# New places for the small pieces of work in a software-pipelined attention block, and value products spread over three rounds

## The chip, the cores and the metric

The kernel runs on one core of a Trainium2 chip. The metric is the device time of one execution in microseconds (us). The kernel before was timed three times: 1149.63, 1153.11 and 1153.94 us, so the median is 1153.11 us.

## The reference, cut to what matters

The input is 16 sequences of 512 tokens with 128 features. A block of attention is followed by a block of experts:

```python
x = x + layernorm(attention(layernorm(x)))        # 16 heads of 8 features, causal
x = x + layernorm(experts(layernorm(x)))          # 1 shared unit of 256, 8 routed experts of 128, top 2

# attention, for each of the 16 heads
scores = (einsum('bhqd,bhkd->bhqk', Q, K) + einsum('bhqd,qkd->bhqk', Q, rel_k[idx])) / sqrt(8)
attn = softmax(where(causal, scores, -1e9))
out = einsum('bhqk,bhkd->bhqd', attn, V) + einsum('bhqk,qkd->bhqd', attn, rel_v[idx])
y = out @ W_o + b_o
```

`idx` clips the distance between two tokens to five values, so only two distances besides the clipped one matter under the causal mask. The change touches the attention block alone.

## The kernel before, in words

**Steps.** The attention block is a pipeline of 19 steps, written out in full. In step t, sequence t is at stage F (first layer norm, queries, keys), sequence t-1 at stage A (scores for the row maxima, values), t-2 at stage B (scores again for the exponentials, their value products) and t-3 at stage C (output projection, second and third layer norm, router logits). Steps 3 to 15 have all four stages; these 13 are called the full steps here. Step 16 has A, B and C, step 17 has B and C, step 18 has C. Then the experts follow.

**Rounds.** A step has 20 rounds, r0 to r19, five for each of four groups of four heads. In each round TensorE (PE) makes two units of scores for stage B (called e units, numbers 0 to 39, tiles `ps_e`) and two for stage A (s units 0 to 39, tiles `ps_s`, with the causal mask added by small products, L1459). ScalarE (ACT) turns an e unit into probabilities (L758), called exp n here. VectorE (DVE) reduces an s unit to row maxima (L1069), called mx n. GpSimd (POOL) clears the masked part of the probabilities (L614), called masks 0 to 19, five for each group.

**Banks.** `ps_e` and `ps_s` have three banks each, used in a fixed ring (`E_RING`, `S_RING`), so a unit on PE waits until the unit three places before it has been read. There is one bank `ps_av` for the value products of a group and one bank `ps_misc` for transposes and other small products, and each use of `ps_misc` waits until the use before it has been read.

**Small pieces.** Between the units stand pieces that occur once or a few times in a step. Their places are numbers: `AT` gives the round before whose units PE does a piece; for the others the places are the ranges of `exps(lo, hi)` on ACT, `maxima(lo, hi)` on DVE and `masks(lo, hi)` on POOL, between which the pieces stand. Each engine works strictly in its own order. The pieces are: q and k (queries, keys; L1497, L1502, copied by ACT L780 to L788); v0 and v1 (values, L1507, read by DVE L1052); e_sums and s_tok (score terms of the two near distances: POOL's `near_products` L626 and L627, PE L1530, ACT L818, PE L1484, DVE L1076); m0 and m1 (row maxima of the two halves of the heads: DVE's `max_half` L1091 to L1102, PE, ACT L843, then a DMA into the stacked queries); `near_half` (POOL L644 to L648, after ACT's exponential L850); av0 to av3 (PE transposes the products of a group, which ACT has copied; DVE's `av_tok_out` L1120 to L1129); oT and oproj (output projection, L1522, DVE's y L1137); `normalise` (POOL L593 to L598); xn2 and logits (L1484, L1563).

**Stacks.** When q and k of a sequence have been split into two halves of float16 (`split`, POOL L620 and L621), SyncE (SP) copies them with 16 DMAs (L457) into the stacked tiles, and then the row maxima with 2 DMAs (L464). The next step's units s0 and e0 wait for these.

**Value products.** `av_part(g, kt)` makes the products of four heads with one block kt of 128 keys: 512, 384, 256 and 128 columns wide for kt 0 to 3. Those of group g stand in the rounds of the next group; those of the last group in the next step. The part kt 0 waits for all five masks of the group and for ACT's copy of the group before.

Of the kernel before, what the change touches and what calls it, by code (L numbers as in the profile page):

```python
# [16 lines left out]
NSEQ, SEQ = 16, 512  # L17
# [25 lines left out]
AT = {"av2": 2, "v1": 2, "e_sums": 3, "s_tok": 4, "v0": 4, "m1": 5, "xT": 5, "av3": 6, "oT": 8, "q": 9,  # L43
      "av0": 9, "k": 10, "oproj": 11, "m0": 13, "av1": 16, "xn2": 18, "logits": 19}
# [176 lines left out]
def block_kernel(nc, x, W_q, b_q, W_k, b_k, W_v, b_v, W_o, b_o, rel_k, rel_v,  # L221
                 router_w, router_bias, sw1, sw3, sw2, ew1, ew2, out):
    ctx = ExitStack()
    with ctx:
# [324 lines left out]
        def _(pool):  # L549
# [101 lines left out]
            def step(st):  # L651
# [5 lines left out]

                if st.B:
                    near_half(st, st.b, 1)
                masks(0, 2)  # L660
# [3 lines left out]
                masks(2, 9)  # L664
                if st.F:
                    split(st)
                masks(9, 12)
# [16 lines left out]
                if st.F:  # L684
                    near_products(st)
# [46 lines left out]
        def _(act):  # L732
# [139 lines left out]
            def step(st):  # L872
# [14 lines left out]
                exps(7, 8)  # L887
                if st.C:
                    av_out(st, st.c, 3)
                if st.A:  # L890
                    v_out(st)
                exps(8, 10)
                if st.B:
                    mT_out(st, st.b, 1)
                if st.F:
                    xT_out(st)
                exps(10, 16)
# [3 lines left out]
                if st.B:  # L901
                    av_out(st, st.b, 0)
                if st.F:
                    q_out(st)
                exps(18, 20)
                if st.F:
# [12 lines left out]
                exps(29, 30)  # L919
                if st.A:  # L920
                    mT_out(st, st.a, 0)
                exps(30, 34)
                if st.F:
                    kd_out(st, 1)
                exps(34, 36)
                if st.C:
                    xn2T_out(st)
                exps(36, 37)
                if st.C:
                    logits_out(st)  # L930
                exps(37, 40)
                if st.B:
                    av_out(st, st.b, 2)
# [41 lines left out]
        def _(dve):  # L975
# [247 lines left out]
            def step(st):  # L1223
# [21 lines left out]
                maxima(4, 5)  # L1245
                if st.A:
                    values_out(st, 1)
                maxima(5, 6)
                if st.F:
                    aggregate(st1, mv1, "stats1")  # L1250
                maxima(6, 7)
                if st.A:
                    s_tok_out(st)
                maxima(7, 8)
                if st.A:
                    values_out(st, 0)
                maxima(8, 13)
                if st.t0 == NSEQ + 1:
                    gates_second(0, EARLY)
                maxima(13, 14)  # L1260
                if st.C:
                    av_tok_out(st, st.c, 3)
                maxima(14, 20)
                if st.B:
                    av_tok_out(st, st.b, 0)
                maxima(20, 21)
# [460 lines left out]
```

## Time and profile before

| what | value |
|---|---|
| median of three runs | 1153.11 us |
| the profiled execution, its own time | 1152.02 us |
| its span in the trace | 1150.2 us |
| PE busy | 949.8 us (83%) |
| DVE busy | 882.9 us (77%) |
| POOL busy | 725.4 us (63%) |
| ACT busy | 696.5 us (61%) |
| DMA | 70.87 MB, mean 62 GB/s |

The shares are means over two different phases. In the slices of the profile the attention block fills the first 30 of 40, with four engines between five and nine tenths busy; the experts fill the last nine, with PE at nine tenths. The span is 1.8 us shorter than the execution's own time.

### The profile page before, as it was taken

The numbers are of one execution on the slowest core, as the hardware profiler recorded it, in microseconds if no ns is written. First come the engines' busy times: TensorE is split into PE (matmuls) and PEld (weight loads), VectorE is DVE, ScalarE is ACT, GpSimd is POOL, SyncE is SP. The second block draws the span as 40 slices with busy tenths as digits, with TensorE's granted clock in tenths as the row PEclk, the third lists the DMA queues.
The fourth block names the chain that finished last, engine by engine and source line by source line (L and its number), as shares of the span: only waits on it lengthen the run. The fifth ranks groups of instructions, "written<-read, shape, count | busy, mean of one in ns | idle before, by whom it ended". The sixth has DMA issues, their size and how long they took to land.

```text
span 1150.2 us, 25409 instructions
## 1 busy us (share of the span) xinstructions
PE 949.8 (83%) x8551; PEld 574.2 (50%) x8551; DVE 882.9 (77%) x2060; ACT 696.5 (61%) x1309; POOL 725.4 (63%) x935
## 2 busy tenths in 40 slices
PE   0368888888898988988888888887737999999996
PEld 0234445444454444544444445453225777777774
DVE  5277888888878888888888888888447877878884
ACT  3425676665666766657576576655505767677763
POOL 2233556748557576575765756736544789889886
PEclk9667999999999999999999999998858999999998
DMA  5100100101001010010100100101122554545451
GB/s 149 43 20 22 38 19 31 35 19 43 20 29 40 19 38 30 20 43 19 36 31 19 46 20 31 34 15 31 47 102 92 151 159 142 171 155 162 142 165 35
DMA packets 61452, 70.87 MB, mean 62 GB/s; under 512 B 9504, under 2 KB 39072, under 8 KB 61344
## 3 DMA queue, kind: packets, MB, share of 16 engines
q1 hardware_dynamic: 61344, 69.47, 19.2%
q8 instruction: 63, 1.03, 0.4%
q14 instruction: 45, 0.37, 0.1%
HBM read 43.75 MB, written 8.65 MB: 46 GB/s over the span
## 4 chain that ended last, share of the span: by engine, by line
PE 43%; DVE 22%; POOL 15%; issue 9%; ACT 7%; SPq 3%; DMA 1%; POOLq 0%; DVEq 0%; ACTq 0%
PE ps_av L1476 7%; PE ps_av L1670 6%; DVE mx L1069 6%; PE ps_s L1637 5%; PE ps_e L1425 4%; PE ps_e L1637 3%; POOL rs L596 3%; POOL y L594 3%; PE ps_s L1448 3%; POOL y L598 3%; PE ps_misc L1484 3%; PE ps_s L1459 2%; DVE mxa L1093 2%; POOL prob L614 2%; DVE st L1028 2%
## 5 line engine op out<-in xcount | busy, mean ns | idle before, releaser
L1069 DVE TENSOR_REDUCE mx<-ps_s 128x1 f32<-128x512 f32 (+2 forms) x640 | 414.9, 683 | 114.3 <-PE ps_s L1459 111.7
L758 ACT ACTIVATE prob<-ps_e 128x512 f32<-128x512 f32 x640 | 351.9, 601 | 166.6 <-PE ps_e L1425 164.7
L614 POOL TENSOR_SCALAR_AFFINE_SELECT prob<-prob 128x516 f32<-128x516 f32 (+1 forms) x320 | 174.0, 568 | 165.1 <-ACT prob L758 163.5
L1448 PE MATMUL ps_s<-ks,qs 63*128 63x512 f16 (+3 forms) x1024 | 230.3, 311 | 51.0 <-DVE mx L1069 28.5
L712 POOL TENSOR_TENSOR hidden_low<-hidden,hidden_high 128x512 fp32r<-128x512 f32 x144 | 191.0, 1354 | 21.5 <-ACT hidden_high L947 20.2
L1425 PE MATMUL ps_e<-qs,ks 64*128 64x512 f16 (+3 forms) x1024 | 190.0, 303 | 9.5 <-ACT prob L758 6.8
L1476 PE MATMUL ps_av<-prob,vp 128*32 128x512 f32 (+3 forms) x2048 | 171.5, 454 | 22.3 <-POOL prob L614 22.3
L1459 PE MATMUL ps_s<-maskb,identb 64*128 64x129 bf16 (+1 forms) x1024 | 141.7, 223 | 0.0
L1459 PE MATMUL ps_s<-maskr,identr 64*128 64x129 bf16 (+1 forms) x1024 | 140.1, 221 | 0.0
L1448 PEld LDWEIGHTS ps_s<-ks,qs 63*128 63x128 f16 x1024 | 79.4, 95 | 105.0 <-DVE mx L1069 70.5
L947 ACT CAST hidden_high<-hidden 128x512 fp32r<-128x512 f32 x160 | 98.0, 613 | 34.8 <-DVE hidden L1373 30.5
L1425 PEld LDWEIGHTS ps_e<-qs,ks 64*128 64x128 f16 x1024 | 59.6, 95 | 114.3 <-ACT prob L758 55.2
L1476 PEld LDWEIGHTS ps_av<-prob,vp 128*32 128x32 f32 x2048 | 54.3, 111 | 91.8 <-issue 42.2
L1373 DVE TENSOR_TENSOR hidden<-gate_rows,ps_e 128x512 f32<-128x512 f32 x96 | 64.2, 684 | 28.3 <-ACT ps_e L962 28.2
L593 POOL TENSOR_SCALAR var<-mv 128x4 f32<-128x4 f32 x48 | 9.8, 203 | 118.0 <-DVE mv L1033 116.6
L1459 PEld LDWEIGHTS ps_s<-maskr,identr 64*128 64x128 bf16 x1024 | 70.7, 97 | 23.0 <-issue 1.5
L1670 PE MATMUL ps_av<-hidden_high,w_high 128*128 128x512 f32 x160 | 69.8, 436 | 9.6 <-POOL hidden_low L712 7.9
L962 ACT ACTIVATE ps_e<-ps_e 128x512 f32<-128x512 f32 x96 | 55.8, 582 | 18.7 <-PE ps_e L1637 18.0
L1459 PEld LDWEIGHTS ps_s<-maskb,identb 64*128 64x128 bf16 x1024 | 61.7, 97 | 6.9 <-issue 0.3
L1670 PE MATMUL ps_av<-hidden_high,w_low 128*128 128x512 f32 x160 | 63.8, 399 | 0.0
L1670 PE MATMUL ps_av<-hidden_low,w_high 128*128 128x512 f32 x160 | 63.4, 397 | 0.0
L644 POOL TENSOR_TENSOR v_near<-v_near,p 128x256 f32<-128x256 f32 x64 | 38.9, 629 | 26.7 <-ACT p L850 26.7
(176 smaller groups left out, 1860.6 us busy)
## 6 DMA issues: line engine op xcount, KB each, us to landing
gate_rows<-gates_dram SPq DMA_DIRECT2D x128, 256.0 KB, 3.5
qs<-qh SPq DMA_DIRECT2D x128, 32.0 KB
qs<-ql SPq DMA_DIRECT2D x128, 32.0 KB
ks<-kh SPq DMA_DIRECT2D x128, 32.0 KB
ks<-kl SPq DMA_DIRECT2D x128, 32.0 KB
xnT_dram<-oT SPq DMA_DIRECT2D x16, 256.0 KB, 2.0
xeT<-xnT_dram SPq DMA_DIRECT2D x16, 256.0 KB, 2.7
out<-result SPq DMA_DIRECT2D x16, 256.0 KB, 2.3
```

The source lines that it names most:

```text
L614: pool.affine_select(out=v, in_=v, compare_op=ALU.is_ge, fill=0.0, base=-2, pattern=cols, channel_multiplier=-1).then_inc(S["p_masked"], 1)
L712: pool.tensor_tensor(hidden_low[hid(f, i)][:, :].bitcast(F32R), hidden[hid(f, i)][:, :], hidden_high[hid(f, i)][:, :], ALU.subtract).then_ ...
L758: act.activation(prob[g % 2][:, u, b, :], ps_e[bank][:, :], ACT.Exp, scale=SCALE).then_inc(S["e_done"], 1)
L947: act.copy(hidden_high[hid(f, i)][:, :].bitcast(F32R), hidden[hid(f, i)][:, :]).then_inc(S["high_ready"], 1)
L1069: dve.tensor_reduce(out, src, AX.X, ALU.max).then_inc(s_free[bank], 1)
L1373: dve.tensor_tensor(hidden[hid(f, i)][:, :], gate_rows[:, k, :], front[k % 4][:, :], ALU.mult).then_inc(S["hidden_ready"], 1)
L1425: last = pe.matmul(scores[:, at:at + WIDTH[kt]], ks[par][rows, pr, P * kt:P * kt + P], qs[par][rows, pr, P * kt:SEQ], start=True, stop=True)
L1448: pe.matmul(scores[:, at:at + P * (qt + 1)], qs[par][rows, 2 * g + off, P * qt:P * qt + P], ks[par][rows, 2 * g + off, 0:P * (qt + 1)], st ...
L1459: last[b] = pe.matmul(both[b][:, lo:hi], eye[rows, :], far[rows, DIAG - (hi - lo):DIAG], start=False, stop=eye is identr)
L1476: last = pe.matmul(ps_av[32 * j:32 * j + 32, P * kt:SEQ], vp[par][:, kt, 4 * g + j, :], prob[g % 2][:, u, j % 2, at:at + w], start=(kt == ...
L1637: last = pe.matmul(out, ws[:, w, :].bitcast(F32R), xs[f.s0 % 2][:, :].bitcast(F32R), start=(j == 0), stop=(j == 2))
L1670: last = pe.matmul(ps_av[:, :], ws[:, w, :].bitcast(F32R), hs[hd][:, :].bitcast(F32R), start=(i % n == 0 and j == 0), stop=(i % n == n - 1 ...
```

## The change

No operation is added or removed. `AT`, the ranges on ACT, DVE and POOL, and the rounds of the value products are changed. The core of the diff:

```diff
-AT = {"av2": 2, "v1": 2, "e_sums": 3, "s_tok": 4, "v0": 4, "m1": 5, "xT": 5, "av3": 6, "oT": 8, "q": 9,
-      "av0": 9, "k": 10, "oproj": 11, "m0": 13, "av1": 16, "xn2": 18, "logits": 19}
+AT = {"e_sums": 1, "av2": 2, "v1": 3, "v0": 5, "m1": 5, "av3": 6, "xT": 6, "s_tok": 7, "oT": 8, "q": 9,
+      "av0": 10, "oproj": 10, "k": 10, "m0": 15, "av1": 17, "xn2": 18, "logits": 19}
...
# POOL: mask 0 now stands ahead of near_half(b, 1); mask 9 ahead of split; near_products from the end to here
                 if st.C:
                     normalise(st, st.c, xn2[:, :, :], tiles(xr[:, st.c, :]), mv3, var3, rs3,
                               "stats3").then_inc(S["xn2_ready"], 1)
+                if st.F:
+                    near_products(st)
                 masks(15, 16)
                 if st.A:
                     near_half(st, st.a, 0)
                 masks(16, 20)
-                if st.F:
-                    near_products(st)
...
# ACT, the start of a step
-                exps(0, 2)
+                exps(0, 1)
+                if st.A:
+                    s_rows_out(st)
+                exps(1, 2)
                 if st.B:
                     p_near_exp(st, st.b, 1)
-                exps(2, 7)
-                if st.A:
-                    s_rows_out(st)
...
# DVE, the middle of a step (after the change)
+                maxima(15, 20)
+                if st.C:
+                    y_out(st)
                 if st.A:
+                    max_half(st, st.a, 0)
+                maxima(20, 21)
                 if st.C:
+                    y_bn(st)
+                    aggregate(st2, mv2, "stats2")
+                maxima(21, 24)
                 if st.B:
                     av_tok_out(st, st.b, 0)
...
# PE, the value products
-                    for kt in {1: (0, 1,), 3: (2, 3,)}.get(u, ()):
+                    for kt in {1: (0,), 2: (1, 2,), 3: (3,)}.get(u, ()):
```

The line numbers of the changed kernel differ by one or two from those of before.

On PE, the end of r9 to the start of r11 in a full step. `wk` is the piece k, `wo` is oproj, `av_s` is av0. Before:

```order
L1459 MATMUL ps_s<-maskr,identr 128x129 x2
L1502 MATMUL ps_e<-xnT,wk 128x512
L1425 MATMUL ps_e<-qs,ks 128x512
L1448 MATMUL ps_s<-ks,qs 128x512
L1425 MATMUL ps_e<-qs,ks 128x512
L1448 MATMUL ps_s<-ks,qs 128x512
L1459 MATMUL ps_s<-maskb,identb 128x129 x2
L1459 MATMUL ps_s<-maskr,identr 128x129 x2
L1522 MATMUL ps_s<-wo,oT 128x128 x4
L1425 MATMUL ps_e<-qs,ks 128x384
```

And after the change:

```order
L1458 MATMUL ps_s<-maskr,identr 128x129 x2
L1521 MATMUL ps_s<-wo,oT 128x128 x4
L1501 MATMUL ps_e<-xnT,wk 128x512
L1483 MATMUL ps_misc<-ident,av_s 128x128 x4
L1424 MATMUL ps_e<-qs,ks 128x512
L1447 MATMUL ps_s<-ks,qs 128x512
L1424 MATMUL ps_e<-qs,ks 128x512
L1447 MATMUL ps_s<-ks,qs 128x512
L1458 MATMUL ps_s<-maskb,identb 128x129 x2
L1458 MATMUL ps_s<-maskr,identr 128x129 x2
```

The output projection has moved one round forward, ahead of the keys, and the transposes av0 one round back; the three stand together ahead of r10.

On DVE, the same place: the reductions mx 18 and 19 (the first row) and what follows. Before:

```order
L1069 TENSOR_REDUCE mx<-ps_s 128x4 x2
L1120 TENSOR_TENSOR den<-ps_misc,p_near 128x16
L1122 TENSOR_TENSOR num<-ps_misc,near 128x128
L1125 RECIPROCAL rden<-den 128x16
L1129 TENSOR_TENSOR o_tok<-num,rden 128x4x32
L1069 TENSOR_REDUCE mx<-ps_s 128x1
L1137 TENSOR_TENSOR y<-ps_s,bo 128x512
L1069 TENSOR_REDUCE mx<-ps_s 128x1
L1091 TENSOR_REDUCE mx<-mx 128x8
L1093 TENSOR_TENSOR mxa<-mx,s_tok 128x4x8
```

And after the change:

```order
L1071 TENSOR_REDUCE mx<-ps_s 128x4 x2
L1139 TENSOR_TENSOR y<-ps_s,bo 128x512
L1093 TENSOR_REDUCE mx<-mx 128x8
L1095 TENSOR_TENSOR mxa<-mx,s_tok 128x4x8
L1097 TENSOR_TENSOR mx<-mxa,s_tok 128x4x8
L1101 TENSOR_SCALAR m<-mx 128x4x8
L1104 SCALAR_TENSOR_TENSOR d<-m,s_tok 128x4x8 x2
L1071 TENSOR_REDUCE mx<-ps_s 128x1
L1030 BN_STATS st<-y 128x6 x4
L1035 BN_AGGR mv<-st 128x2 x4
```

y and the maxima of the first half stand ahead of mx 20, the statistics of y directly behind it, and `av_tok_out` of av0 behind mx 23 (it stood behind mx 19).

On POOL, from the third layer norm of a step to the first masks of the next. Before:

```order
L598 TENSOR_TENSOR y<-y,rs 128x512
L614 AFFINE_SELECT prob<-prob 128x4x129
L644 TENSOR_TENSOR v_near<-v_near,p 128x4x64 x2
L645 TENSOR_TENSOR p_near<-p 128x4x8
L648 TENSOR_TENSOR near<-v_near 128x4x64
L614 AFFINE_SELECT prob<-prob 128x2x128
L614 AFFINE_SELECT prob<-prob 128x4x129 x2
L614 AFFINE_SELECT prob<-prob 128x2x128
L626 TENSOR_TENSOR e<-kd,qf 128x512
L627 TENSOR_TENSOR e<-kd,qf 128x511
L644 TENSOR_TENSOR v_near<-v_near,p 128x4x64 x2
```

And after the change:

```order
L598 TENSOR_TENSOR y<-y,rs 128x512
L626 TENSOR_TENSOR e<-kd,qf 128x512
L627 TENSOR_TENSOR e<-kd,qf 128x511
L614 AFFINE_SELECT prob<-prob 128x4x129
L644 TENSOR_TENSOR v_near<-v_near,p 128x4x64 x2
L645 TENSOR_TENSOR p_near<-p 128x4x8
L648 TENSOR_TENSOR near<-v_near 128x4x64
L614 AFFINE_SELECT prob<-prob 128x2x128
L614 AFFINE_SELECT prob<-prob 128x4x129 x2
L614 AFFINE_SELECT prob<-prob 128x2x128
L614 AFFINE_SELECT prob<-prob 128x4x129
L644 TENSOR_TENSOR v_near<-v_near,p 128x4x64 x2
```

The two near products now stand ahead of masks 15 to 19, and mask 0 of the next step ahead of that step's first `near_half`.

## Rows read from the trace of the kernel before

**Rows 1.** Engines by stretch: a full step, step 16, the experts.

```profile
core 0: us, PE busy (x) PEld busy (x) DVE busy (x) ACT busy (x) POOL busy (x), PEclk, DMA share, GB/s
319.63:366.65 47.02, 40.84 (x465) 22.41 (x465) 39.11 (x97) 30.68 (x61) 30.36 (x45) 1.00 0.09 30
743.20:788.00 44.80, 39.12 (x466) 21.48 (x462) 37.30 (x89) 26.70 (x54) 25.09 (x40) 1.00 0.06 20
...
863.00:1150.20 287.20, 264.00 (x1121) 203.85 (x1121) 221.59 (x455) 187.45 (x339) 229.06 (x192) 0.97 0.44 137
```

**Rows 2.** Timeline of PE, full steps: start, length, instruction, idle before.

```profile
366.65 0.39 PE L1425 MATMUL ps_e<-qs,ks 64*128 64x512 f16 x1
...
383.81 1.71 PE L1476 MATMUL ps_av<-prob,vp 128*32 128x512 f32 x16
385.46 0.28 PE L1425 MATMUL ps_e<-qs,ks 64*128 64x256 f16 x1
...
387.52 0.86 PE L1476 MATMUL ps_av<-prob,vp 128*32 128x256 f32 x16
388.31 1.13 PE L1497 MATMUL ps_e<-xnT,wq 128*128 128x512 f32 x2
...
390.79 1.12 PE L1502 MATMUL ps_e<-xnT,wk 128*128 128x512 f32 x2
...
392.50 1.16 PE L1522 MATMUL ps_s<-wo,oT 128*128 128x128 f32 x8
...
395.04 0.23 PE L1448 MATMUL ps_s<-ks,qs 63*128 63x128 f16 x1 [0.89 <-DVE mx L1069]
```

**Rows 3.** Timeline of DVE, full steps.

```profile
352.04 0.36 DVE L1033 BATCH_NORM_AGGREGATE mv<-st 128x2 f32<-128x6 f32 x4
...
368.54 0.17 DVE L1091 TENSOR_REDUCE mx<-mx 128x8 f32<-128x24 f32 x1
368.74 1.30 DVE L1093 TENSOR_TENSOR mxa<-mx,s_tok 128x32 f32<-128x32 f32 x1
...
371.55 0.68 DVE L1069 TENSOR_REDUCE mx<-ps_s 128x1 f32<-128x512 f32 x1
...
380.22 0.69 DVE L1052 TENSOR_TENSOR v_near<-ps_s,dv 128x512 f32<-128x512 f32 x1 [0.72 <-ACT vp L804]
...
386.34 2.53 DVE L1069 TENSOR_REDUCE mx<-ps_s 128x2 f32<-128x512 f32 x4 [0.41 <-PE ps_s L1459]
390.69 1.29 DVE L1069 TENSOR_REDUCE mx<-ps_s 128x4 f32<-128x512 f32 x2 [1.82 <-PE ps_s L1459]
```

**Rows 4.** Timeline of POOL, full steps.

```profile
352.59 0.19 POOL L593 TENSOR_SCALAR var<-mv 128x4 f32<-128x4 f32 x1 [2.60 <-DVE mv L1033]
...
359.13 0.19 POOL L593 TENSOR_SCALAR var<-mv 128x4 f32<-128x4 f32 x1
...
362.62 0.65 POOL L614 TENSOR_SCALAR_AFFINE_SELECT prob<-prob 128x516 f32<-128x516 f32 x1
...
368.72 1.27 POOL L626 TENSOR_TENSOR e<-kd,qf 128x512 f32<-128x512 f32 x1
369.95 1.09 POOL L627 TENSOR_TENSOR e<-kd,qf 128x511 f32<-128x511 f32 x1
```

**Rows 5.** Every mxa of `max_half` on DVE: least, median, greatest in ns.

```profile
L1093 DVE TENSOR_TENSOR mxa<-mx,s_tok x32: 191/620/1303, 73.2 to 789.8; 128x32 f32<-128x32 f32 x32
```

**Rows 6.** Chain of waits of step 2: start, length, what.

```profile
112.70 1.14 PE ps_e L1502 x2
```

**Rows 7.** Timeline of SP, end of step 2: stacks, row maxima.

```profile
117.77 1.44 SPq L457 DMA_DIRECT2D qs<-qh  x2
...
129.25 1.25 SPq L464 DMA_DIRECT2D qs<-mT  x2
```

**Rows 8.** Timeline of PE, start of step 3.

```profile
131.75 0.37 PE L1425 MATMUL ps_e<-qs,ks 64*128 64x512 f16 x1
```

**Rows 9.** Timeline of ACT, full steps.

```profile
371.67 0.26 ACT L850 ACTIVATE p<-d 128x64 f32<-128x64 f32 x1 [2.63 <-DVE d L1102]
```

More of the change, by code:

```diff
@@ L656, in masks @@
                         mask_tiles(st, lo, hi)
+                masks(0, 1)
                 if st.B:
                     near_half(st, st.b, 1)
-                masks(0, 2)
+                masks(1, 2)
                 if st.F:
@@ L663, in step @@
                               "stats1").then_inc(S["xn_ready"], 1)
-                masks(2, 9)
+                masks(2, 10)
                 if st.F:
                     split(st)
-                masks(9, 12)
+                masks(10, 12)
                 if st.C:
@@ L905, in step @@
                 exps(18, 20)
+                if st.B:
+                    av_out(st, st.b, 0)
                 if st.F:
@@ L1245, in step @@
                 maxima(4, 5)
+                if st.F:
+                    aggregate(st1, mv1, "stats1")
+                maxima(5, 6)
                 if st.A:
                     values_out(st, 1)
[L1248 to L1251, printed above, removed]
+                maxima(6, 10)
+                if st.A:
+                    values_out(st, 0)
+                maxima(10, 11)
+                if st.C:
+                    av_tok_out(st, st.c, 3)
+                maxima(11, 13)
+                if st.t0 == NSEQ + 1:
+                    gates_second(0, EARLY)
+                maxima(13, 15)
                 if st.A:
                     s_tok_out(st)
-                maxima(7, 8)
+                maxima(15, 20)
+                if st.C:
+                    y_out(st)
                 if st.A:
[L1256 to L1260, printed above, removed]
+                    max_half(st, st.a, 0)
+                maxima(20, 21)
                 if st.C:
-                    av_tok_out(st, st.c, 3)
-                maxima(14, 20)
+                    y_bn(st)
+                    aggregate(st2, mv2, "stats2")
+                maxima(21, 24)
                 if st.B:
                     av_tok_out(st, st.b, 0)
-                maxima(20, 21)
-                if st.C:
-                    y_out(st)
-                maxima(21, 22)
-                if st.A:
-                    max_half(st, st.a, 0)
-                maxima(22, 23)
-                if st.C:
-                    y_bn(st)
-                maxima(23, 24)
-                if st.C:
-                    aggregate(st2, mv2, "stats2")
                 maxima(24, 25)
@@ L1286, in step @@
                     aggregate(st3, mv3, "stats3")
-                maxima(31, 32)
+                maxima(31, 36)
                 if st.B:
                     av_tok_out(st, st.b, 1)
-                maxima(32, 40)
+                maxima(36, 40)
                 own.end()
```

27 lines of the change are left out of this document (13 added, 14 removed).

## The prediction

> **What bounds the kernel now.** I read the busy time by stretch first. The 13 full steps last 47.0 us each with PE busy for 40.8 and DVE for 39.1 [rows 1]: neither is full, so a step loses about 6 to 8 us in which the two wait for each other. The experts take 287 us with PE at 92% and are not touched. So what the change is worth is read from one full step, times 13, and a little for step 16 (44.8 us).
>
> The timelines of that step show who waits. Positions below count from the step's first e unit, at 366.65 [rows 2]; rows before that time belong to the step that began at 319.63, one period earlier. Three kinds of loss are to be seen. First, DVE's `max_half` of the second half takes 3.0 us (368.54 to 371.55) though its first small operation can take 0.19: it takes 1.30 here, beside POOL's near product of 1.27 [rows 3 to 5]. ACT sits idle for 2.63 until the result is there [rows 9], and PE, three banks ahead at most, stops too. Second, PE works in lumps: 1.65 for kt 0 and 1 (383.81 to 385.46), then two rounds and a transposition in 2.06, then 0.79, then queries, av0 and keys in a row, while DVE waits 1.82 for its next scores [rows 2, 3]. Third, right behind that, DVE has the lump: y, `max_half` and the statistics, and now PE waits 0.89 for DVE [rows 2]. Both wait, in turn, because the lumps of one do not stand beside the lumps of the other.
>
> **The change part by part.** I walk one full step in the new order. Lengths: a round is 0.73 us of PE (two rounds and a transposition of 0.6 make 2.06), the products 1.65 and 0.79 a group, by columns 0.94, 0.71, 0.53 and 0.26 for kt 0 to 3; mx is 0.6 (four in 2.53) [rows 2, 3].
>
> *Start of the step to the keys.* Before, k begins at 24.1 (390.79) [rows 2]. PE's own work ahead of it is 10 rounds, 7.3; products of two groups, 4.9; and small pieces: two value products of 1.1 each, queries 1.1, e_sums 1.0, four transposes (av2, av3, xT, oT) and av0 at 0.6, s_tok and m1 together 0.7. That makes 20.2, so 3.9 is waiting. Now av0 (0.6) leaves this stretch and oproj (1.16 in its row, 1.1 net) enters: 20.7. The waits:
> - `near_products` leaves the end of POOL's step, and with it the two operations of 1.27 and 1.09 that stood beside `max_half` (368.72 to 371.04) [rows 4]. In their place come masks of half a us. No row has exactly this overlap. Below, all small operations at their least length make about 1.3; above, it stays at 3.0. The nearest case is `max_half` of the first half, whose mxa has the median of 0.62 [rows 5] beside masks: 2.2. I take 2.2, so DVE gains 0.8. DVE then has mx 5 and the values of v1 done at 9.75, not 10.6.
> - PE waits there still: s5 needs mx 2, done at 6.05, where PE could be at 5.2. This, the wait of e2 for ACT in r1 and 0.3 for POOL's masks are nearly all that is left: 1.8.
> - v0, one round later, meets DVE with mx 8 and 9 done as well. DVE waits for ACT's copy as before (0.72 at 380.22, which is position 13.6) [rows 3]; now it is done at 13.45 with two more reductions behind it and s_tok still ahead, 1.5 ahead of before.
> - From r6 to r10 PE works without a stop: kt 0 at 14.8, kt 1 and 2 after r7, kt 3 after r8, then q, r9, oproj. k begins at 22.5, 1.6 earlier though it has 0.5 more ahead of it.
>
> *The middle.* mx 19 ends at 22.75 and oproj at 22.5, so y follows without the wait of 1.82. While DVE does y and `max_half` (2.8), PE does k, av0 (2.3 in all with the transposes) and r10: lump beside lump. From here DVE is the bound. Its work: y 0.6, `max_half` 2.2, 16 reductions 9.6, statistics and aggregate of y 1.25 and of x 1.3, av_tok of av0 0.9, and the first 0.3 of that of av1. Sum 16.15, so av1's bank is read at 38.9. Then PE has xn2 0.6, r18, kt 3, logits 1.0 and r19: 3.4. The next step begins at 42.3 to 42.4.
>
> *New waits.* The transposes xn2 share a bank with av1, and av1 is now read behind mx 35, not mx 31: xn2 cannot start before 38.9. This costs about 0.5, since PE arrives at 38.5; it is in the sum. Behind it on ACT stands the copy of xn2, now ahead of exp 35, so exps 35 to 39 start at 40.2 and exp 39 ends 1.25 after the new start (before, 1.1). ACT's copy of e_sums stands ahead of exp 1 and waits for PE's r0; that falls into the 2.63 in which ACT was idle anyway [rows 9]. If that cover went, it would cost 0.6.
>
> *POOL.* The statistics of y end at 27.3, not 32.7 (352.04 and four short operations) [rows 3], so POOL no longer waits 2.60 for them [rows 4]; it waits for exp 23 instead and begins the second norm at 28.6. From there it has no gap: norm and addition 4.8, three masks 1.6, third norm 3.6, near products 2.4, mask 15, `near_half` 2.2, four masks 2.1, in all 17.3 to 17.5, ending 3.7 after the next start (before, 2.1: at 368.72 the masks are done [rows 4]). PE wants the last group's kt 0 at 2.85. The wait of 0.85 is mostly hidden behind s5, which waits till 6.05 anyway.
>
> *SP.* From k to the next e0 there is a fixed chain: copies, `split`, 16 DMAs, 2 DMAs, landing. Step 2 is bound by it: k at 112.70, stacks from 117.77, row maxima from 129.25, e0 at 131.75, so 19.05 [rows 6 to 8]. Before, 24.1 + 19.05 = 43.2 leaves 3.8 in hand. Now 22.5 + 19.05 = 41.55: 0.8 in hand. This is the floor, and it moves with k.
>
> So the walk gives 42.4. Such a walk leaves out small delays, and three chains (DVE with PE, POOL, SP) now end within 1 us of each other, so I add 0.6: 43.0. Gain 4.0 x 13 = 52, and 1.5 for step 16, which has neither k nor split. Steps 1 and 2 hang on SP, steps 17 and 18 are sparse: nothing counted. The profiled execution took 1152.0 us itself (span 1150.2 and 1.8 around it), 1.1 below the median of the runs, which is within their spread. 1152 - 54 = 1098 us.
>
> **Rivals.**
> - *DVE and POOL keep holding each other.* The row shows mxa at 1.30 beside a POOL operation of 1.27, and at 0.19 at its least [rows 3 to 5]. POOL now has no gap around the start of a step. If the pieces of `near_half` (0.6 and 0.7) slip under `max_half` of the second half, this stays at 3.0, 0.8 more than in the sum: 43.8 a step, gain 3.2 x 13 + 1.5 = 43, so 1109 us. Against it: by the walk `near_half` is over 2.1 before the masks end, and `max_half` stands beside masks. The Trainium skill (SBUF — State Buffer, section "SBUF: two separate sides") calls the port pair of VectorE and GpSimd "an exclusive lock, not a bandwidth split", held for the whole instruction. By that rule every small operation waits for the end of whatever POOL is in, and a gapless POOL speaks against this change; the 1.30 beside 1.27 agrees.
> - *POOL's tail decides.* For it: 17.4 us without a gap, and near products of 2.4 put ahead of the masks that kt 0 waits for. Against: its start moves forward by more than 4. If POOL slips by a further 2.3 (its near products' length), the masks end at 6.0, kt 0 at 6.95, and s5, r2 and all behind come 2.0 later: 45.0 a step. 1152 - 26 - 1.5 = 1124 us.
> - *The shared bank makes it slower.* One chain: mx 35, reading of av1, xn2, copy, exp 35 to 39. Before, mx 35 ends at about 43.5 with av1 already read. If the stretches ahead gain nothing while DVE takes mx 20 and av0's piece behind y, mx 35 still ends at 43.5 and the next start is 3.6 later, 47.1: break-even. It turns slower once mx 35 is later than that. With DVE delayed by 1.6 through the longer overlap with POOL: 48.7 a step, 1152 + 22 = 1174 us. Against it: my walk has mx 35 at 38.6, five us earlier.
> - *Nothing moves.* The 3.9 of waits return elsewhere, at ACT or at SP. Against it: SP's floor is 43.2 even with k at its old place. 1152 us.
>
> **How the numbers follow.** Forecast 0.49 (alone, steps of 42.2 to 44.5, so 1088 to 1118); the held `max_half` 0.15; POOL's tail 0.22; nothing moves 0.05; the bank 0.09. The two sides of the sum are 1.3 and 3.0 for `max_half` (0.9 a step down, 0.8 up). The range of 8 in 10 takes the forecast, with the low end moved down for `max_half` at 1.3, and the tail with some room: 1084 to 1140. A measurement of this kernel tells about 0.5% (6 us) from no change. Faster 0.86, same 0.05, slower 0.09.
>
> **What would show it.** In the profile of the changed kernel: full steps of about 43 us; mxa of the second half near 0.6; no wait of DVE over 1 us ahead of r10; xn2 on PE waiting for DVE's num; the last masks of a step ending 3 to 4 us into the next; e0 beginning within 1 us of the landing of the row maxima. Wrong would be: steps over 45 us with PE's products waiting for POOL (the tail), or PE's xn2 waiting more than 2 us for DVE (the bank).

## The result, and the profile after

| | before | after |
|---|---|---|
| median, timed together (4 runs each) | 1152.35 us | 1089.43 us |
| its range | 1149.63 to 1153.94 | 1086.63 to 1092.70 |
| profiled execution, own time (span) | 1152.02 (1150.2) | 1092.7 (1090.6) |

The ratio is 0.9457, with a 95% interval of 0.9425 to 0.949: 63 us faster, where 55 were forecast (1098 us; 1089.4 lies in the range given). The profiled execution of after is at the slow edge of its runs, so between the two profiled executions it is 59.3 us (59.6 of span).

The busy times on the page of after:

```profile
PE 945.4 (87%) x8551; PEld 557.6 (51%) x8551; DVE 854.2 (78%) x2060; ACT 693.6 (64%) x1309; POOL 725.9 (67%) x935
```

PE's work is what it was (945 for 950 us), and the span is 60 us shorter: what went is waiting. DVE's busy time fell by 29 us though it has the same instructions; this is time in which an instruction was on DVE but was held, 27 us of it in `max_half` (1.2 and 0.85 us shorter in each of 13 steps, shown below).

By stretch (columns as in [rows 1]), one full step and the experts of after:

```profile
342.80:386.00 43.20, 40.90 (x466) 21.44 (x464) 37.06 (x97) 30.51 (x61) 30.45 (x46) 1.00 0.10 33
...
805.20:1090.60 285.40, 262.58 (x1121) 202.94 (x1121) 222.53 (x455) 187.10 (x338) 228.87 (x192) 0.98 0.45 138
```

Against [rows 1] the step has the same 40.9 us of PE in 43.2 us instead of 47.0: PE now has 2.3 us of gaps, and no longer 6.2. Where the 59.6 us of span went, with the logits products and the first e unit as marks:

| stretch | before | after | gain |
|---|---|---|---|
| start to step 3 (131.75, 127.59) | 131.75 | 127.59 | 4.2 |
| from there to the logits of step 15 (741.77, 686.77): 13 steps | 610.0 | 559.2 | 50.8 |
| logits of 15 to those of 16 | 44.65 | 40.85 | 3.8 |
| to those of 17, then 18 | 74.59 | 75.37 | -0.8 |
| on to the experts' first product | 2.2 | 2.2 | 0 |
| experts | 287.0 | 285.4 | 1.6 |

The experts are unchanged, so their 1.6 us are a difference between two executions and not the change's.

The timeline of PE in the step that begins at 342.60 (start, length, instruction, idle before), to be laid beside [rows 2]:

```profile
342.60 0.38 PE L1424 MATMUL ps_e<-qs,ks 64*128 64x512 f16 x1
...
346.24 1.06 PE L1475 MATMUL ps_av<-prob,vp 128*32 128x512 f32 x8 [0.42 <-POOL prob L614]
...
364.32 1.16 PE L1521 MATMUL ps_s<-wo,oT 128*128 128x128 f32 x8
365.31 1.02 PE L1501 MATMUL ps_e<-xnT,wk 128*128 128x512 f32 x2
...
382.57 0.63 PE L1483 MATMUL ps_misc<-ident,y 128*128 128x128 f32 x4 [0.81 <-POOL y L598]
...
385.82 0.37 PE L1424 MATMUL ps_e<-qs,ks 64*128 64x512 f16 x1
```

oproj and k stand in a row, av0 right behind them, and the next step begins 43.22 after this one. PE's only waits of more than 0.2 us in it are 0.42 (346.24), 0.25 (348.58) and 0.81 (382.57).

DVE in the same step, beside [rows 3]:

```profile
344.65 0.17 DVE L1093 TENSOR_REDUCE mx<-mx 128x8 f32<-128x24 f32 x1
344.86 0.40 DVE L1095 TENSOR_TENSOR mxa<-mx,s_tok 128x32 f32<-128x32 f32 x1
...
346.47 0.68 DVE L1071 TENSOR_REDUCE mx<-ps_s 128x1 f32<-128x512 f32 x1
...
364.43 1.29 DVE L1071 TENSOR_REDUCE mx<-ps_s 128x4 f32<-128x512 f32 x2 [0.90 <-PE ps_s L1458]
...
366.44 0.30 DVE L1095 TENSOR_TENSOR mxa<-mx,s_tok 128x32 f32<-128x32 f32 x1
...
369.45 0.38 DVE L1035 BATCH_NORM_AGGREGATE mv<-st 128x2 f32<-128x6 f32 x4 [0.16 <-DVE st L1030]
...
381.83 0.28 DVE L1124 TENSOR_TENSOR num<-ps_misc,near 128x128 f32<-128x128 f32 x1
```

`max_half` of the second half takes 1.82 us (344.65 to 346.47), where it took 3.0 in [rows 3]; mxa, its second operation, 0.40 instead of 1.30. In the middle DVE's wait for scores is 0.90 and no longer 1.82; but the wait before that one grew from 0.41 to 0.82 (362.24), so the two together only fell from 2.23 to 1.72.

POOL at both ends of that step, beside [rows 4]:

```profile
344.18 2.00 POOL L614 TENSOR_SCALAR_AFFINE_SELECT prob<-prob 128x256 f32<-128x256 f32 x4
...
381.39 1.04 POOL L598 TENSOR_TENSOR y<-y,rs 128x512 f32<-128x512 f32 x1
382.39 1.33 POOL L626 TENSOR_TENSOR e<-kd,qf 128x512 f32<-128x512 f32 x1
383.69 1.08 POOL L627 TENSOR_TENSOR e<-kd,qf 128x511 f32<-128x511 f32 x1
```

The near products now run at 382.39 to 384.77, ahead of the last masks, and those end 3.6 into the step (346.18).

### The profile page after: what moved, and what is told of

The parts are those of the page before. It is cut to its first block and busy times, and to the rows that moved or that the text cites. A ratio compares the mean times of both kernels' runs of the same rounds, so it can differ in the third digit from the quotient of the medians.

```text
span 1090.6 us, 25410 instructions
## 1 busy us (share of the span) xinstructions
PE 945.4 (87%) x8551; PEld 557.6 (51%) x8551; DVE 854.2 (78%) x2060; ACT 693.6 (64%) x1309; POOL 725.9 (67%) x935
## 5 line engine op out<-in xcount | busy, mean ns | idle before, releaser
L1424 PE MATMUL ps_e<-qs,ks 64*128 64x512 f16 (+3 forms) x1024 | 185.3, 303 | 9.1 <-DMA qs<-mT 4.4
L1475 PE MATMUL ps_av<-prob,vp 128*32 128x512 f32 (+3 forms) x2048 | 181.5, 450 | 9.3 <-POOL prob L614 9.3
L1424 PEld LDWEIGHTS ps_e<-qs,ks 64*128 64x128 f16 x1024 | 54.8, 95 | 101.8 <-ACT prob L759 66.4
L1458 PEld LDWEIGHTS ps_s<-maskr,identr 64*128 64x128 bf16 x1024 | 76.0, 97 | 21.5 <-issue 1.4
L1475 PEld LDWEIGHTS ps_av<-prob,vp 128*32 128x32 f32 x2048 | 47.6, 110 | 59.3 <-issue 28.0
L1458 PEld LDWEIGHTS ps_s<-maskb,identb 64*128 64x128 bf16 x1024 | 64.8, 96 | 8.6
L596 POOL TENSOR_TENSOR rs<-var,neg_half 128x4 f32<-128x4 f32 x48 | 49.6, 1033 | 3.8
L1483 PEld LDWEIGHTS ps_misc<-ident,av_s 128*128 128x128 f32 x256 | 27.8, 144 | 45.7 <-issue 43.6
```

The costliest lines, as they stand in the source:

```text
L1424: last = pe.matmul(scores[:, at:at + WIDTH[kt]], ks[par][rows, pr, P * kt:P * kt + P], qs[par][rows, pr, P * kt:SEQ], start=True, stop=True)
L1458: last[b] = pe.matmul(both[b][:, lo:hi], eye[rows, :], far[rows, DIAG - (hi - lo):DIAG], start=False, stop=eye is identr)
L1475: last = pe.matmul(ps_av[32 * j:32 * j + 32, P * kt:SEQ], vp[par][:, kt, 4 * g + j, :], prob[g % 2][:, u, j % 2, at:at + w], start=(kt == ...
```

## The experiments

All twelve were timed against the kernel before on the same chip, in three sessions on three chips (median of before 1151.4, 1151.8 and 1151.4). After was not timed again in them, so "dearer than after" compares across sessions. Steps and waits come from one profiled execution of each kernel. "Step" is the mean of the twelve distances between the logits products of steps 3 to 15, and in brackets that of those steps in which the granted clock stayed at 1.00 (2.4 GHz). One difference is in some of them besides the one named: in minus_values, minus_near, minus_mid, minus_end and esums_late ACT's copy of av2 stands behind that of the logits, with the same exps on both sides. minus_end, which has it together with its own moves, is 0.17 us a step longer than after, so it costs at most about that.

| kernel | median (range) | ratio, 95% | step |
|---|---|---|---|
| before | 1152.4 (1149.6 to 1153.9) | | 47.08 |
| after | 1089.4 (1086.6 to 1092.7) | 0.943 to 0.949 | 43.24 |
| near_only (added to before) | 1132.5 (1131.0 to 1133.5) | 0.980 to 0.985 | 45.59 |
| plus_mid (added to before) | 1131.6 (1129.6 to 1132.5) | 0.980 to 0.985 | 45.86 |
| near_mid (both) | 1114.1 (1111.8 to 1114.4) | 0.965 to 0.969 | 44.42 |
| minus_near (taken from after) | 1140.8 (1135.6 to 1144.4) | 0.986 to 0.992 | 46.81 (45.57) |
| esums_late | 1109.7 (1106.2 to 1111.4) | 0.959 to 0.966 | 44.48 (44.29) |
| minus_mid | 1124.8 (1122.2 to 1129.6) | 0.975 to 0.981 | 45.33 (44.90) |
| minus_values | 1109.4 (1104.8 to 1109.6) | 0.959 to 0.965 | 44.13 (44.11) |
| minus_spread | 1109.1 (1103.5 to 1112.9) | 0.961 to 0.968 | 44.34 (43.63) |
| minus_end | 1089.1 (1088.0 to 1090.0) | 0.943 to 0.948 | 43.41 |
| sp_plus4 | 1097.5 (1096.9 to 1100.1) | 0.952 to 0.956 | 43.48 (43.35) |
| x1_early | 1105.7 (1100.3 to 1110.5) | 0.957 to 0.962 | 44.37 (43.49) |
| x1_t1_early | 1102.9 (1100.7 to 1103.2) | 0.956 to 0.959 | 44.34 (43.04, one step) |

**Near products ahead of the last masks, alone (near_only).** POOL, in the kernel before:

```diff
+                if st.F:
+                    near_products(st)
                 masks(15, 16)      # then values of near_half, masks(16, 20)
-                if st.F:
-                    near_products(st)
```

> The kernel before with one edit: the near products ahead of mask 15 on POOL. Port theory: max_half of the second half falls from 3.0 to about 2.0 us and the step by 0.5 to 1.2 us, 47.0 to about 46.1: 1136 to 1145 us. Rival 'the other waits take its place' (PE in r5 to r10 is held by ACT's and PE's own lumps, which stay): under 0.3 us a step, 1148 us or more.

Measured: 1132.5, 20 us faster than before and more than expected (1136 to 1145), and steps 1.49 shorter. DVE in this kernel, a second half and the first half behind it:

```profile
363.20 0.17 DVE L1090 TENSOR_REDUCE mx<-mx 128x8 f32<-128x24 f32 x1
363.40 0.53 DVE L1092 TENSOR_TENSOR mxa<-mx,s_tok 128x32 f32<-128x32 f32 x1
...
388.33 0.61 DVE L1092 TENSOR_TENSOR mxa<-mx,s_tok 128x32 f32<-128x32 f32 x1
...
389.34 0.58 DVE L1098 TENSOR_SCALAR m<-mx 128x32 f16<-128x32 f32 x1
```

The second half begins at 363.20, and from there to the end of d it takes 1.65, where 2.0 was expected (3.10 in before, read in the same way). `max_half` lost 1.45 and the step 1.49: this stretch is on the path in full, and one move on POOL is a third of the change. The rows from 388.33 are of the first half, which is as in before: 2.27 in all.

**The middle alone, and both (plus_mid, near_mid).** In the kernel before: oproj at round 10 ahead of k, av0 at 10; DVE takes y, `max_half`, mx 20 and the statistics of y in the new order, POOL has mask 9 ahead of `split`, ACT copies av0 in its new place.

```diff
-      "av0": 9, "k": 10, "oproj": 11,
+      "av0": 10, "k": 10, "oproj": 10,
                 # POOL
-                masks(2, 9)
+                masks(2, 10)
                 # DVE
-                maxima(22, 23)
+                maxima(20, 21)
                 # y_bn(st), aggregate, maxima(21, 24), then av_tok_out(st, st.b, 0)
```

> The kernel before with the middle of the step alone as after: oproj and av0 in r10, y and the first half's max_half ahead of mx 20, statistics of y behind it, av0's piece behind mx 23, split behind mask 9. Lump theory: DVE's wait of 1.82 us and PE's of 0.89 go, 1.2 to 2 us a step as its removal cost, 1125 to 1137 us. Rival: the parts only work together (what PE gains in the middle it waits for POOL's tail at the end), under 0.7 us a step, 1142 us or more.

> The kernel before with both edits that were run alone: the near products ahead of mask 15 (alone, the step fell from 47.0 to 45.6) and the middle of the step as changed (alone, 45.9). Lump theory: two separate places, so the gains add to 2.6 us: 44.2 to 44.8 us a step, 1110 to 1120 us. Rival 'one shared wait' (each alone frees the same chain): steps above 45.2 us, 1125 us or more. Rival 'only together' (the parts help one another, since taking them out one at a time cost 1.8 and 3.2 or more): below 44.0 us, 1108 us or less.

Measured: 1131.6 and 1114.1, both in the range expected. The middle alone gives 1.22 us a step, and the first half's `max_half` goes from 2.28 to 1.42. Here is DVE in plus_mid, where the near products were left in their place, first in a second half, then in a first:

```profile
361.21 1.31 DVE L1092 TENSOR_TENSOR mxa<-mx,s_tok 128x32 f32<-128x32 f32 x1
362.56 1.01 DVE L1094 TENSOR_TENSOR mx<-mxa,s_tok 128x32 f32<-128x32 f32 x1
...
384.75 0.31 DVE L1092 TENSOR_TENSOR mxa<-mx,s_tok 128x32 f32<-128x32 f32 x1
```

The second half still has 1.31 and 1.01, one for each near product, while the first has 0.31. The gains add: 1.49 and 1.22 make 2.71, and near_mid has 2.66. They are two places that do not depend on each other, and together they bring 38 of the 63 us.

What in the middle brings its 1.22 is less clear, for three things changed there at once. First, `max_half` of the first half is 0.85 shorter. In before it stood beside `split`:

```profile
394.51 1.17 POOL L621 TENSOR_TENSOR kl<-kf,kh 128x512 f16<-128x512 f32 x1
...
395.11 0.62 DVE L1093 TENSOR_TENSOR mxa<-mx,s_tok 128x32 f32<-128x32 f32 x1
```

The POOL operation ends at 395.68 and mxa at 395.73. Second, PE no longer waits 0.44 and 0.79 for POOL's masks ahead of two kt 0. This is the first of the two, in before:

```profile
396.10 1.71 PE L1476 MATMUL ps_av<-prob,vp 128*32 128x512 f32 x16 [0.44 <-POOL prob L614]
```

Third, the lumps: DVE's wait of 1.82 only fell to 1.38, and PE's wait of 0.89 for DVE went, while another of 0.75 came up a little later:

```profile
346.05 0.39 PE L1445 MATMUL ps_s<-ks,qs 63*128 63x512 f16 x1 [0.75 <-DVE mx L1068]
```

No run changes one of the three alone. So it is shown that the new middle brings 1.22 a step, and only argued that lump beside lump is the reason.

**The same two, taken from after (minus_near, esums_late, minus_mid).** minus_near has the near products at the end of POOL's step again, e_sums in round 3 and its ACT copy behind exp 6. esums_late has only the last two of these. minus_mid undoes the middle.

```diff
-AT = {"e_sums": 1, "av2": 2,
+AT = {"av2": 2, "e_sums": 3,
                 # minus_near also, on POOL, behind masks(16, 20):
+                if st.F:
+                    near_products(st)
```

> The changed kernel with the near products back at the end of POOL's step, e_sums in r3 and ACT's copy of them behind exp 6. Port rival: max_half of the second half goes back to 3.0 us or more and most of the gain goes with it, 2.5 us a step or more, 1122 us and up. Lump theory: max_half gets 0.8 to 1.2 us longer but is only one of four places; 0.7 to 1.4 us a step, 1099 to 1108 us.

> The changed kernel with e_sums in r3 and ACT's copy of them behind exp 6, as before, but with the near products kept early on POOL. It splits the run that undid both and lost 51 us. Port theory: max_half of the second half stays at 1.8 us (it was 3.1 there, beside the near products), and the step stays below 43.9 us: 1090 to 1098 us without clock drops. Rival 'lump': kt 1 and 2, e_sums and v1 in a row while DVE waits for v1 were the loss; steps of 44.5 us or more, 1106 us or more.

> The changed kernel with the middle of the step as before: oproj in r11, av0 in r9, y behind mx 20, the first half's max_half behind mx 21, statistics of y behind mx 22 and 23, av0's piece on DVE behind mx 19, split ahead of mask 9. Lump theory: DVE waits again for PE ahead of r10 and PE for DVE in r11; 1.2 to 2 us a step, 1105 to 1116 us. Rival 'port' (the gain is that max_half no longer stands beside the near products): under 0.5 us a step, below 1097 us.

Measured: 1140.8, 1109.7 and 1124.8; so 51, 20 and 35 us dearer than after. minus_near is far above the 1099 to 1108 expected, and esums_late too came out as its rival said (1106 or more): in it DVE waits 0.94 for the product of v1 (317.48) and PE 0.85 for POOL's masks (311.33), 0.42 in after. minus_mid is above its 1105 to 1116; falls of the clock are 5 us of it. minus_near's order costs 2.3 us a step (1.05 of them e_sums, the rest 1.28, where near_only gained 1.49), and nine of its twelve steps have 1.6 on top. DVE, POOL and PE in one of these, first DVE:

```profile
363.96 1.22 DVE L1096 TENSOR_TENSOR mx<-mxa,s_tok 128x32 f32<-128x32 f32 x1
365.22 1.01 DVE L1100 TENSOR_SCALAR m<-mx 128x32 f16<-128x32 f32 x1
```

Beside them on POOL:

```profile
363.86 1.28 POOL L625 TENSOR_TENSOR e<-kd,qf 128x512 f32<-128x512 f32 x1
365.09 1.09 POOL L626 TENSOR_TENSOR e<-kd,qf 128x511 f32<-128x511 f32 x1
```

The first of these operations of DVE ends at 365.18 and the first product at 365.14; the second ends at 366.23 and the second product at 366.18. Each of these small operations of DVE lasts until the POOL operation beside it ends. Then PE:

```profile
367.21 0.28 PE L1447 MATMUL ps_s<-ks,qs 63*128 63x256 f16 x1 [1.19 <-DVE mx L1070]
...
368.58 0.28 PE L1447 MATMUL ps_s<-ks,qs 63*128 63x256 f16 x1 [0.81 <-DVE mx L1070]
...
369.38 2.36 PE L1475 MATMUL ps_av<-prob,vp 128*32 128x384 f32 x16
```

and the windows of this kernel (the number behind POOL's count is the granted clock), two whole periods from logits to logits and then one microsecond of the second:

```profile
314.05:359.63 45.58, 41.75 (x469) 21.79 (x465) 38.40 (x98) 29.98 (x61) 30.69 (x46) 1.00 0.09 31
359.63:406.82 47.19, 43.39 (x468) 22.18 (x464) 38.39 (x98) 29.96 (x61) 30.62 (x46) 0.96 0.09 30
370.00:371.00 1.00, 1.00 (x12) 0.39 (x8) 1.00 (x6) 0.00 (x0) 1.00 (x3) 0.50 0.10 34
```

PE waited 1.19 and 0.81 for DVE, the clock went to 0.50 (1.2 GHz), and the sixteen products took 2.36, where they took 1.28 in the step before, behind the same two waits. So PE is "busy" for 1.6 more and the period is 1.6 longer. This is a price that my prediction did not have. The parts of the change, taken away one at a time (near, middle, values, spread), cost 126 us together, twice the 63 that all of them bring. By the profiled executions the clock is about 28 of the 63 too many: 9 steps at 1.6 here, 3 at about 1.7 in minus_mid, and 12 times 0.71 (44.34 less 43.63) in minus_spread. The rest was not taken apart; that waits which two parts remove together come back with either is my reading, not shown.

**Values and their copies (minus_values).** v1 in round 2, v0 and s_tok in 4, xT in 5, their copies on DVE and ACT, and masks 0 and 1 ahead of `near_half`.

```diff
-      "v1": 3, "v0": 5, "m1": 5, "av3": 6, "xT": 6, "s_tok": 7,
+      "v1": 2, "v0": 4, "s_tok": 4, "m1": 5, "xT": 5, "av3": 6,
```

> The changed kernel with the first half of the step as before: v1 in r2, v0 and s_tok in r4, xT in r5, with their places on ACT and DVE, and near_half ahead of mask 0. e_sums stays in r1. Lump theory: PE's pieces crowd r2 to r5 again while DVE has max_half; 0.7 to 1.5 us a step, 1099 to 1109 us. Rival 'port': under 0.5 us a step, below 1097 us.

Measured: 1109.4, at the upper edge of the range expected (1109); 0.87 a step and 5.2 us ahead of the logits of step 3. In a full step PE now waits 1.06 for POOL's first norm ahead of xT (320.55); in after it does not wait there at all (356.04).

**Value products in three rounds (minus_spread).**

```diff
-                    for kt in {1: (0,), 2: (1, 2,), 3: (3,)}.get(u, ()):
+                    for kt in {1: (0, 1,), 3: (2, 3,)}.get(u, ()):
```

> The changed kernel with the value products of a group back in two rounds (kt 0 and 1, then kt 2 and 3); all else as changed. Lump theory (PE and DVE lose time where the lumps of one do not stand beside the lumps of the other; several places share the gain): the lump of 1.65 us is partly hidden, since DVE is the bound from r10 to r17; 0.3 to 0.7 us a full step, 1093 to 1099 us. Rival 'one cause': if spreading the products were the cause, steps of over 45 us and 1115 us or more.

Measured: 1109.1, above what was expected. The order alone costs the 0.4 us a step that was expected (43.63). The rest is the clock: in four of the twelve steps the clock fell for a while, and these last 44.7 to 47.5.

**The end of the step (minus_end).** m0 at 13, av1 at 16, DVE reads av1 behind mx 31, ACT's copies in their old places: the shared bank of the transposes xn2 as before.

```diff
-      "m0": 15, "av1": 17, "xn2": 18,
+      "m0": 13, "av1": 16, "xn2": 18,
                 # DVE
-                maxima(31, 36)
+                maxima(31, 32)
```

> The changed kernel with the end of the step as before: m0 in r13, av1 in r16, av1's piece on DVE behind mx 31, ACT's copy of xn2 behind exp 35, logits behind exp 36, av2's copy last. Lump theory: this takes the bank wait of xn2 away (PE waits 0.8 us there, but for POOL's third norm as well) and puts PE's av1 and DVE's piece back beside their old neighbours; small either way, 43.0 to 43.9 us a full step, 1086 to 1100 us. Rival 'bank' (from the prediction): reading av1's bank behind mx 35 is a cost that the change carries, so undoing it gives 0.5 us a step or more, 1083 us or less.

Measured: 1089.1, no difference to after. Full steps are 0.17 longer (2 us in all), and steps 17 and 18 are 5.1 us shorter together (39.92 and 30.38 for 42.05 and 33.32). But those two steps vary by 3 us from one execution to the next: sp_plus4, esums_late and x1_t1_early, with the new places at the step's end, take 72.2 to 72.5 for both, and after 75.4. So the wait at the bank neither costs nor brings anything that these runs can tell.

**Room on SP (sp_plus4).** Four further DMAs of 16 KB on SP in every step, into memory that nothing reads, behind the first half's stacks and ahead of the row maxima.

```diff
+                    for i in range(4):
+                        sp.dma_start(scratch[...], wv[0:32, :]).then_inc(S["scratch"], 16)
```

> The changed kernel with four more DMAs of 16 KB on SP in each step, behind the 16 of the first half's stacks and ahead of the row maxima; they copy a constant into memory that nobody reads, all else as changed. In the profile the row maxima have been issued at 383.0 and e0 begins at 385.8, a landing of at most 1.25 us after the issue leaves 1.5 us in hand. Floor theory: four issues take 2.8 us, so the step grows by 1.0 to 1.6 us: 1102 to 1112 us. Rival 'SP has room' (the landing is much quicker or e0 not held by it): under 0.3 us a step, below 1094 us.

Measured: 1097.5, less dear than expected. SP in two of its full steps, with the four issues and the row maxima behind them, and the next step's first e unit on PE:

```profile
299.33 1.83 SPq L494 DMA_DIRECT2D scratch<-wv  x4
301.28 1.26 SPq L464 DMA_DIRECT2D qs<-mT  x2
303.79 0.37 PE L1427 MATMUL ps_e<-qs,ks 64*128 64x512 f16 x1
...
429.75 2.84 SPq L494 DMA_DIRECT2D scratch<-wv  x4
432.71 1.26 SPq L464 DMA_DIRECT2D qs<-mT  x2
435.22 0.37 PE L1427 MATMUL ps_e<-qs,ks 64*128 64x512 f16 x1 [1.61 <-DMA qs<-mT]
```

and the row maxima of the step shown above, in after:

```profile
381.75 1.25 SPq L464 DMA_DIRECT2D qs<-mT  x2
```

In after they are out at 383.00, the next e unit begins at 385.82, and landing takes 1.25 at most [rows 7, 8]: 1.6 us in hand. In sp_plus4 this is used up. In every full step the first e unit begins 1.25 behind the end of the issue (302.54 and 303.79, 433.97 and 435.22), so SP holds it there. What the sum missed is that such a delay is taken up again: in the first of the two steps shown the unit begins 0.3 later than in after, counted from k, and the step stays as it was (43.26); in the second it begins 1.8 later, and the step is 0.5 longer (43.79). So in after SP does not bound a full step, and a delay beyond the 1.6 costs less than its length. The medians differ by 8 us, the two profiled executions by 4.2. Of these, 4.1 stand ahead of the logits of step 3 (part of them through a fall of the clock from 130.60 to 134.01), and the 2.8 of the full steps are offset by steps 17 and 18, which vary by as much. Ahead of step 3 SP does set the pace, in the kernel after too, whose PE waits for it at the start of steps 2 and 3:

```profile
87.08 0.58 PE L1424 MATMUL ps_e<-qs,ks 64*128 64x512 f16 x1 [3.07 <-DMA qs<-mT]
...
108.41 1.13 PE L1501 MATMUL ps_e<-xnT,wk 128*128 128x512 f32 x2 [0.57 <-ACT qf L782]
...
127.59 0.37 PE L1424 MATMUL ps_e<-qs,ks 64*128 64x512 f16 x1 [1.37 <-DMA qs<-mT]
```

From k to the next e unit it is 19.2 here, and 19.05 in the kernel before [rows 6, 8]; in the full step above it is 17.7 from k (365.31) to the end of the issue and at most 1.25 for landing, so the chain has the same length there.

**A try for more (x1_early, x1_t1_early).** Since DVE is the bound behind r10, statistics of x and av1's reading one or two reductions earlier should free xn2 earlier.

```diff
-                maxima(25, 31)
+                maxima(25, 30)
                 # x1_bn(st), aggregate
-                maxima(31, 36)
+                maxima(30, 34)      # x1_early: maxima(30, 36)
                 # av_tok_out(st, st.b, 1)
```

> The changed kernel with only the statistics of x one reduction earlier. Lump theory: POOL's norm gives up 0.6 us, but then av1's bank holds xn2, read at about 382.7 with the statistics now ahead of everything behind them: 0 to 0.3 us a step, 1085 to 1090 us. Rival: POOL's norm alone holds xn2, then this run is as fast as the one with both edits.

> The changed kernel with two DVE places moved: the statistics of x ahead of mx 30 (not 31) and av1's piece ahead of mx 34 (not 36). In the changed kernel xn2 begins at 382.57, held by POOL's third norm (382.43) and by the reading of av1's bank (about 382.1), and PE could be there at 381.7. Lump theory: both come 0.6 to 0.8 us earlier, so the step falls from 43.24 to 42.5 to 42.9: 1080 to 1087 us. Rival 'other chain' (SP's chain from k, or POOL's masks at the start of the next step, takes over at once): within 0.2 us a step, 1087 to 1091 us.

Measured: 1105.7 and 1102.9, slower than after by 13 to 16, where 0 to 9 faster was expected. The first full step of x1_t1_early took 43.04, 0.2 less than after; all later ones, each with a fall of the clock in it, 44.4 to 44.7. In a later step, PE:

```profile
337.05 0.23 PE L1447 MATMUL ps_s<-ks,qs 63*128 63x128 f16 x1 [1.23 <-DVE mx L1070]
...
337.94 1.93 PE L1475 MATMUL ps_av<-prob,vp 128*32 128x512 f32 x8
...
339.80 1.01 PE L1483 MATMUL ps_misc<-ident,av_s 128*128 128x128 f32 x4
```

and two windows of one microsecond, in the wait and behind it:

```profile
336.00:337.00 1.00, 0.00 (x0) 0.00 (x0) 0.97 (x6) 1.00 (x3) 0.60 (x3) 1.00 0.11 34
...
338.00:339.00 1.00, 1.00 (x9) 0.13 (x8) 1.00 (x2) 0.00 (x0) 1.00 (x1) 0.50 0.10 33
```

The same two pieces in after:

```profile
377.99 1.06 PE L1475 MATMUL ps_av<-prob,vp 128*32 128x512 f32 x8
378.99 0.66 PE L1483 MATMUL ps_misc<-ident,av_s 128*128 128x128 f32 x4
```

With the statistics one reduction earlier (on DVE from 335.01, four in 0.86), PE's next scores wait 1.23 for a bank, the clock is at 0.50 right behind that wait, and the products take 1.93 for 1.06, the transposes 1.01 for 0.66. That is 1.2 of the 1.4 that a step lost. The order itself may be a little better than that of after; the falls of the clock make it worse. No kernel tried here beats after.

Do the waits bring the falls? Here is the longest wait of PE in the full steps of each kernel (it recurs in every one to within 0.05 us, and sp_plus4, where it does not, is left out), and in how many of the twelve the clock fell:

| kernel | longest wait of PE, us | steps with a fall |
|---|---|---|
| after | 0.81 | 0 |
| near_only, plus_mid, near_mid | 0.94 | 0 |
| before | 0.94 | 2 |
| esums_late | 0.85 | 3 |
| minus_values | 1.06 | 1 |
| minus_end | 1.13 | 0 |
| minus_near | 1.19 | 9 |
| x1_early | 1.22 | 7 |
| x1_t1_early | 1.22 | 11 |
| minus_mid | 1.60 | 3 |
| minus_spread | 1.66 | 4 |

Falls are frequent only in kernels with a wait of 1.19 or more, but a longer wait does not mean more of them, and steps with the same waits have one or have none. That the wait is the cause is therefore not shown; no run changes a wait and nothing else.

## Why the prediction was right, point by point

- **What bounds it.** `max_half` of the second half, held by POOL's near products, is on the path in full: shown by near_only (1.45 of wait, 1.49 of step). The new middle brings 1.22, and the two add (near_mid). That lumps which do not stand beside each other are its reason was not shown: in the same place a second hold on `max_half` and two waits for POOL's masks went too. The other 1.18 a step of the change (44.42 to 43.24) were only measured by taking parts out, e_sums 1.05, values 0.87 and spread 0.39, which sum to more.
- **The walk through a step.** 42.4 plus 0.6 against 43.22. Its checkpoints, from the step's start: k 22.5, measured 22.7 (365.31); aggregate of y 27.3, measured 27.2 (369.45 and its 0.38); av1's bank read 38.9, measured 39.5 (381.83 and its 0.28); xn2 38.9, measured 39.97; end of POOL's masks 3.7, measured 3.6. Late are the reading of the bank, by 0.6, and xn2, by 1.1: it waits 0.81, and the last to be ready is POOL's third norm (382.43), 0.3 behind DVE's reading of the bank (382.11), and not that reading, as I had it. The 0.6 that I added for three chains that end together has about the size of this delay.
- **`max_half`, mis-sized.** I took 2.2 for both halves. Measured: 1.8 to 1.9 and 1.4, so `max_half` was put 1.2 a step too long. I had read the first half of before (2.2) as the length that masks give. Its mxa of 0.62 stood beside `split` and ended with it (395.73 and 395.68, above), and the whole goes from 2.28 to 1.42 when only the middle is rearranged (plus_mid). So 2.2 was not the price of masks, and for the first half the low bound of 1.3 was the nearer one. With the measured lengths the walk would have given 41.2. The step is 43.22, so what the walk leaves out is 2.0 and not 0.6. Two errors cancel, and that 43.0 came so near is in part luck. Where the 2.0 stand was not taken apart.
- **13 full steps.** 52 forecast, 50.8 measured.
- **Step 16.** 1.5 forecast, 3.8 measured: as much as a full step. I had left out that `max_half`, the values and av0 are in it as in the others; only k, keys and split are missing. The parts weigh differently there than in a full step, though: near_only gains 0.6 and plus_mid 2.3.
- **Steps 1 and 2.** Nothing forecast, 4.2 measured. "Steps 1 and 2 hang on SP" was true and the conclusion was not. SP's chain is a fixed distance from k, and k is not fixed: it comes 1.3 earlier in step 1, step 2 begins 2.2 earlier (89.30 and 87.08), k in step 2 comes 4.3 earlier (112.70, 108.41), and step 3 begins 4.2 earlier. In step 1 the clock helped too. The same product, k of step 1, in before:

```profile
68.93 2.07 PE L1502 MATMUL ps_e<-xnT,wk 128*128 128x512 f32 x2
```

and in after:

```profile
67.64 1.12 PE L1501 MATMUL ps_e<-xnT,wk 128*128 128x512 f32 x2
```

From 50 to 70 us the granted clock was 0.67 in before and 1.00 in after. The missing 0.95 and the 1.29 are the 2.2 by which step 2 begins earlier. One execution is not enough for the exact amount: x1_early, whose steps 0 to 2 are those of after, begins step 3 at 128.93 and not at 127.59.

- **Steps 17 and 18.** Nothing forecast, 0.8 lost. These two steps vary by 3 us between kernels with the same places at the step's end (minus_end, above), so the 0.8 says nothing. In the full steps the new places at the end bring 0.17 each.
- **SP's floor.** I had 0.8 us in hand, and expected e0 within 1 us of the landing; it was 1.6. Past that, a delay of the first e unit reaches the step only in part (sp_plus4).
- **Rivals.** *Held `max_half`*: not so, 1.8 to 1.9 and not 3.0. The Trainium skill (SBUF — State Buffer, section "SBUF: two separate sides") has the lock last as long as the whole instruction; minus_near agrees, with DVE's 1.22 and 1.01 ending 0.04 and 0.05 behind the two products. "Every small operation" in the prediction was too wide: the reduction at the head of `max_half` took 0.17 beside a mask too (368.54). The lock did not speak against the change, because the long operations went elsewhere. *POOL's tail*: kt 0 waits 0.42 for POOL (346.24 above), not more. *The bank*: xn2 waits 0.81, and taking the old places back changed nothing. *Nothing moves*: no.
- **What was not in the prediction at all.** The clock. Before loses it in two of twelve full steps (0.4 each), after in none. As the forecast went it mattered little, but it decides variants: minus_near, minus_spread and both x1 kernels stand well above what their order costs.

**Open.** Which of the three things in the middle brings its 1.22; why the clock falls in nine steps of minus_near and not in the others, though the waits ahead of it are alike; how much of the 5.2 us ahead of step 3's logits in minus_values is the order (2.6 of them stand ahead of k of step 1, where the granted clock from 50 to 70 us was 0.75 and not 1.00); and what the order of x1_t1_early would take if the clock held (one step of 43.04 is all there is; thirteen of them would make about 1086 to 1087, an estimate).

## What to carry to other kernels

Where two engines wait for each other in turn, walk one period engine by engine in the new order before you build it: here that gave the step within 0.3 us, though two errors of over 1 us cancelled in it. Putting the lumps of the two side by side went with a gain of 1.22 us a step, but other waits went in the same edit. Keep long element-wise operations of POOL away from a chain of short ones on DVE that others wait for, since each short one that is held then lasts until the long one ends. Judge a reordering by the granted clock in its steps too, and don't price a part by taking it out alone: two parts added to before gave their sum within 0.05 us a step, while the parts taken out summed to twice the whole.

## What the runs showed that I had not expected

- A wait of PE of about 1.2 us can be followed at once by a granted clock of 0.50, and this costs 1.4 to 1.6 us a time (x1_t1_early, minus_near); the same wait in other steps is followed by none. PE then shows more busy time, not less: 43.39 for 41.75.
- It is not only sum and product of two tensors that are held. A conversion of 128x32 to half precision took 0.18 when POOL stood elsewhere, 0.58 beside masks (389.34) and 1.01 beside a near product (365.22).
- Reductions of DVE that read PSUM kept their length beside every POOL operation: all 640 of before and of after took 0.65 to 0.70.
- Issues on SP that push the row maxima out by 1.9 us cost a step of 43 us nothing; where they push them out by 3.4 us, it is 0.5 longer.
